# Causal attention of a two-layer kernel: two heads over the 128 rows of the array, masks added in VectorE's maximum

## The chip, the cores and the metric

The kernel runs on one NeuronCore of a Trainium2 chip. The time is the device time of one execution, in microseconds (us); three runs of the kernel before gave 1619.24, 1622.28 and 1633.52, median 1622.28.

## The reference, cut to what matters

Two transformer layers over X of 4 x 512 tokens and 256 features. Only the attention of the first layer, and the projection in front of it, are touched:

```python
Xn = (X - mu) * rsqrt(var + EPS) * ln_g + ln_b
Q, K, V = (split_heads(Xn @ W + b) for W, b in ((Wq, bq), (Wk, bk), (Wv, bv)))   # 16 heads of 16 features
scores = einsum('bhqd,bhkd->bhqk', Q, K) / sqrt(16)
scores = where(causal, scores, -inf)
A = softmax(scores, axis=-1)
AV = einsum('bhqk,bhkd->bhqd', A, V)        # then heads side by side, @ Wo + bo
```

After it come a feed-forward part with decoded 4-bit weights, a second attention (4 groups of features, no mask), and 64 experts of which each token takes 6.

## The kernel before, in words

A program of blocks. In a block each engine (PE is TensorE, DVE VectorE, ACT ScalarE, POOL GpSimd, SP the engine that issues most DMAs) has its own list of instructions, in order, and semaphores written by hand join them. The blocks that matter:

**make_constants** loads X on SP; POOL sets an identity matrix and `mask_q`, a 128 x 128 triangle of 0 and -1e30.

**project_qkv** goes over four chunks of 512 tokens (`chunks`). Each chunk is normalized on DVE (for chunk c+1 while chunk c is multiplied), transposed and multiplied on PE. Q and K are each written as a high part `hi` (fp32r, by ACT, L297) and a remainder `lo` (by DVE, L262), and V with a column of ones. SP stores them (L212, L215): per chunk four DMAs of 512 KB for `hi` and `lo` of Q and K, and one of 1 MB for V. `hi` and `lo` have one buffer each: ACT and DVE wait on `qk_stored` before they overwrite them for the next chunk. The next block starts only when all stores have landed.

**attention** (`att` in the rows) works on 16 units, each 512 tokens by 4 heads. Four buffers (SLOTS) hold the stacks of a unit. A stack holds, at 16 partitions each, the parts of Q (hi, lo, hi, lo) and of K (hi, hi, lo, lo), so that one product over them gives the whole product of the sums; eight DMAs of 128 KB load them (L461). Rows 96 and 97 hold the negated row maximum in two parts against ones in K's stack. A unit runs through these steps:

- `scores_q`: PE makes scores with queries over the partitions, block row i (128 queries) by (i+1)*128 keys, 11 groups of heads in two banks of `ps_1`, in the order i = 2, 1, 0, 3. A second matmul (L568) adds the mask on the diagonal block of each head.
- `maxima` (L701): DVE reduces a group to the row maximum. `split_maxima` (L710, L712) negates and splits it, PE turns it (`turn_maxima`, into its own bank `ps_tr`), ACT copies it, and SP writes it into Q's stack in two DMAs (L476).
- `scores_k` (L586): PE makes the transposed scores, maximum subtracted, two heads per step; `exps` on ACT (L661) takes the exponential of both at once; POOL zeroes the masked triangle (L535).
- `values` (L600): PE multiplies with V, four heads beside each other in four groups of 32 columns. ACT copies the output, PE turns it (`turn_output`), DVE normalizes it, SP stores it.

The order on PE is written by hand (`body`): one body works on four units at once, between steps of the scores_q of units u and u+1 stand those of the scores_k of u-1 and the values of u-2 and u-1. `scores_q` waits on `max_done` for a free bank; the first `scores_k` of a unit waits on `neg_loaded`, the DMAs of the maxima.

Of the kernel before, what the change touches and what calls it, by code (L numbers as in the profile page):

```python
# [7 lines left out]
F32 = mybir.dt.float32  # L8
F32R = mybir.dt.float32r
# [4 lines left out]
ALU = mybir.AluOpType  # L14
# [35 lines left out]

def make_constants(nc, x_dram, x_sb, ident, ident_bf, mask_q):

    with ExitStack() as ctx:
# [11 lines left out]
        @block.gpsimd  # L65
        def _(pool):
            for t in (ident, ident_bf, mask_q):
                pool.memset(t[:, :], 0.0).then_inc(filled, 1)
            pool.wait_ge(filled, 3)
# [4 lines left out]
            pool.affine_select(out=mask_q[:, :], in_=mask_q[:, :], compare_op=ALU.is_ge, fill=NEG, base=0,  # L74
                               pattern=[[-1, P]], channel_multiplier=1).then_inc(shaped, 1)
            pool.wait_ge(shaped, 3)

# [73 lines left out]

def project_qkv(nc, tag, x_sb, ident, w, affine, q_dram, k_dram, v_dram, heads, pitch):

# [5 lines left out]
    with ExitStack() as ctx:  # L159
# [33 lines left out]
        block = ctx.enter_context(nc.Block())  # L193
        NQ = 2 * KD

        @block.sync
        def _(sp):
# [10 lines left out]
            def body(c, more):  # L208
                for j, dst in enumerate((q_dram, k_dram)):
                    sp.wait_ge(lo_done, c * NQ + (j + 1) * KD)  # L210
                    for part, t in enumerate((hi, lo)):
                        sp.dma_start(dst[part].rearrange("(k p) t -> p k t", p=P)[:, :, bass.ds(c * CHUNK, CHUNK)],  # L212
# [5 lines left out]
            chunks(sp, body)  # L218
            sp.wait_ge(qk_stored, 16 * 4 * NCH)
            sp.wait_ge(v_stored, 16 * NCH)  # L220
# [10 lines left out]
        def _(dve):  # L231
# [23 lines left out]
            def body(c, more):  # L255
                if more:
                    norm(c + 1)
                wait(dve, qk_stored, c * 64)
                for n in range(NQ):
# [19 lines left out]
        def _(act):  # L279
# [10 lines left out]
            def body(c, more):  # L290
                if more:
                    roots(c + 1)
                wait(act, qk_stored, c * 64)
                for n in range(NQ):
# [1514 lines left out]
def program(nc, a, y):  # L1809

    with ExitStack() as ctx:
# [3 lines left out]
        ident_bf = s.sbuf("ident_bf", [P, P], BF16)  # L1815
        mask_q = s.sbuf("mask_q", [P, P], BF16)
        q_dram = nc.dram_tensor("q_parts", [2, D, T], F32, kind="Internal").ap()
        k_dram = nc.dram_tensor("k_parts", [2, D, T], F32, kind="Internal").ap()
# [3 lines left out]
        make_constants(nc, a["L0_attn_X"], x_sb, ident, ident_bf, mask_q)  # L1822

        for layer, heads, pitch, causal, parts in ((0, 16, 32, True, PARTS_16), (1, 4, 66, False, PARTS_64)):
# [4 lines left out]
            project_qkv(nc, f"qkv{layer}", x_sb, ident, w, affine, q_dram, k_dram, v_dram, heads, pitch)  # L1829
            attention(nc, f"att{layer}", ident, ident_bf, mask_q, q_dram, k_dram, v_dram, att_dram,  # L1830
                      heads, pitch, causal, parts, scale)
            if layer == 1:
# [51 lines left out]
```

## Time and profile before

| | us |
|---|---|
| three runs | 1619.24, 1622.28, 1633.52 |
| the profiled execution | 1626.69 |
| its span, first to last instruction | 1625.0 |
| projection of layer 0, up to the first load of attention | to 89.3 |
| causal attention | 89.3 to about 308 |

The profile is one execution. Busy time is what an engine spends in instructions; waits are put down to the engine or DMA whose event ended them. PE matmuls are pipelined and their ends modelled, so a busy PE may still not stream columns all the time. "Granted clock" is 1.00 for 2.4 GHz and 0.50 for 1.2 GHz.

### The profile page before, as it was taken

The page shows a single profiled execution, that of the slowest core. Times are in us where ns is not written, and L with a number is a line of the kernel's source. Part 1 is how long each engine was busy: PE and PEld are TensorE (multiplying, and loading weights), DVE is VectorE, ACT ScalarE, POOL GpSimd, SP SyncE. Part 2 cuts the span into 40 slices and gives each one's busy share as a digit, 9 for nine tenths or more (in the row PEclk, how much of TensorE's full clock was granted, in tenths as well). Part 3 has the DMA queues.
Part 4 walks back from the last instruction along what each step waited for, and adds up shares of the span by engine and source line. Part 5 has one row for each costly group of instructions (what it writes and reads, how often), then busy time and mean ns, then how long its engine had stood idle before and what let it go on. Part 6 is the DMA issues. An engine that isn't in the chain of part 4 may idle for free. (4 is left out here: it accounts for less than half of the span.)

```text
span 1625.0 us, 23544 instructions
## 1 busy us (share of the span) xinstructions
PE 1295.9 (80%) x6028; PEld 905.4 (56%) x6028; DVE 781.8 (48%) x2451; ACT 378.8 (23%) x746; POOL 383.9 (24%) x478
## 2 busy tenths in 40 slices
PE   4859999648799999796997647910999999999960
PEld 2435555436688887653554534510677677767640
DVE  6746666277412212253442564401555555655546
ACT  1205455333211212021332111100222222222210
POOL 0042222432100000001000204774233333333320
PEclk9959999879999999998999758965899999999985
DMA  3598786411980000055442201223999999999959
GB/s 109 219 178 115 119 124 94 101 52 63 295 266 1 0 0 0 23 195 174 128 132 71 69 1 56 103 110 113 276 309 308 296 299 298 312 294 297 299 177 323
DMA packets 189717, 260.04 MB, mean 160 GB/s; under 512 B 43887, under 2 KB 119375, under 8 KB 189655
## 3 DMA queue, kind: packets, MB, share of 16 engines
q1 hardware_dynamic: 141847, 190.33, 43.2%
q10 hardware_dynamic: 35568, 34.74, 7.3%
q0 software_dynamic: 12240, 34.23, 5.9%
q8 instruction: 29, 0.48, 0.1%
q14 instruction: 33, 0.27, 0.1%
HBM read 173.11 MB, written 85.78 MB: 159 GB/s over the span
## 5 line engine op out<-in xcount | busy, mean ns | idle before, releaser
L1553 PE MATMUL experts_ps_gu<-experts_wgu,experts_xt 128*128 128x352 f32 x636 | 218.4, 466 | 4.1 <-DMA experts_wgu<-L_ffn_w_gate_up 3.0
L1689 POOL DMA_INDIRECT y_parts<-experts_y,experts_at x159 | 152.6, 960 | 290.9 <-DVE experts_y L1645 287.9
L701 DVE TENSOR_REDUCE att_mx<-att_ps 128x1 f32<-128x512 f32 (+3 forms) x240 | 151.9, 654 | 135.4 <-PE att_ps L568 67.1
L564 PE MATMUL att_ps<-att_ks,att_qs 96*128 96x512 f32 (+4 forms) x384 | 157.3, 475 | 30.0 <-DMA att_ks<-k_parts 27.2
L1574 PE MATMUL experts_ps_y<-experts_wd,experts_ht 96*128 96x256 f32 x636 | 164.0, 380 | 0.0
L1596 ACT ACTIVATE experts_xt<-experts_ps_x 128x256 f32<-128x256 f32 x159 | 61.1, 384 | 417.1 <-PE experts_ps_x L1542 409.8
L661 ACT ACTIVATE att_pt<-att_ps 128x1024 f32<-128x1024 f32 (+3 forms) x160 | 121.9, 766 | 134.5 <-PE att_ps L586 134.3
L1553 PEld LDWEIGHTS experts_ps_gu<-experts_wgu,experts_xt 128*128 128x128 f32 x636 | 121.1, 192 | 49.1 <-DMA experts_wgu<-L_ffn_w_gate_up 4.3
L564 PEld LDWEIGHTS att_ps<-att_ks,att_qs 96*128 96x128 f32 (+1 forms) x384 | 78.3, 207 | 94.3 <-issue 61.4
L1542 PE MATMUL experts_ps_x<-all_ident,experts_x 128*128 128x128 f32 x318 | 64.6, 285 | 70.6 <-DMA experts_x<-x_sorted 70.6
L1383 POOL DMA_INDIRECT x_sorted<-all_rows,moe_slots x96 | 96.8, 1008 | 92.1 <-DVE moe_slots L1376 63.1
L586 PE MATMUL att_ps<-att_qs,att_ks 128*128 128x512 f32 (+3 forms) x384 | 109.4, 382 | 8.9 <-DMA att_qs<-att_neg_t 7.9
L1574 PEld LDWEIGHTS experts_ps_y<-experts_wd,experts_ht 96*128 96x128 f32 x636 | 109.9, 193 | 8.8
L600 PE MATMUL att_ps_o<-att_pt,att_vs 128*32 128x512 f32 (+4 forms) x640 | 112.9, 475 | 0.5 <-POOL att_pt L535 0.5
L1031 PE MATMUL mlp_ps_y<-mlp_w_down,mlp_inner 128*128 128x256 f32 x512 | 112.3, 382 | 0.8 <-DVE mlp_inner L949 0.8
L1031 PEld LDWEIGHTS mlp_ps_y<-mlp_w_down,mlp_inner 128*128 128x128 f32 x512 | 97.7, 191 | 14.9 <-DVE mlp_inner L949 1.3
L1655 DVE SCALAR_TENSOR_TENSOR experts_placed<-experts_x,experts_owner,experts_part 128x6 f32<-128x6 f32 x159 | 35.2, 222 | 128.7 <-DMA y_parts<-experts_y,experts_at 128.5
L949 DVE TENSOR_TENSOR mlp_inner<-mlp_gs,mlp_ps_u 128x512 f32<-128x512 f32 x64 | 43.8, 687 | 98.4 <-PE mlp_ps_u L1021 93.6
L1542 PEld LDWEIGHTS experts_ps_x<-all_ident,experts_x 128*128 128x128 f32 x318 | 50.5, 201 | 71.6 <-DVE experts_hid L1674 70.9
L1563 PEld LDWEIGHTS experts_ps_h<-all_ident,experts_hid 128*96 128x96 f32 x318 | 47.7, 173 | 72.4 <-DVE experts_hid L1630 54.3
L535 POOL TENSOR_SCALAR_AFFINE_SELECT att_pt<-att_pt 128x256 f32<-128x256 f32 x128 | 52.0, 407 | 143.6 <-ACT att_pt L661 143.4
L586 PEld LDWEIGHTS att_ps<-att_qs,att_ks 128*128 128x128 f32 x384 | 63.8, 196 | 35.1 <-issue 12.3
(202 smaller groups left out, 2051.5 us busy)
## 6 DMA issues: line engine op xcount, KB each, us to landing
experts_wgu<-L_ffn_w_gate_up SPq DMA_DIRECT2D x159, 352.0 KB, 5.6
experts_wd<-L_ffn_w_down SPq DMA_DIRECT2D x159, 176.0 KB
experts_x<-x_sorted ACTq DMA_DIRECT2D x159, 136.0 KB, 5.3
x_sorted<-mlp_w_empty SPq DMA_DIRECT2D x26, 816.0 KB, 10.6
att_qs<-q_parts SPq DMA_DIRECT2D x112, 128.0 KB, 3.3
att_ks<-k_parts SPq DMA_DIRECT2D x112, 128.0 KB, 5.3
combine_got<-y_parts ACTq DMA_DIRECT2D x24, 512.0 KB, 9.5
q_parts<-qkv_hi SPq DMA_DIRECT2D x8, 512.0 KB, 2.9
```

The lines of the kernel that those rows point to most:

```text
L564: ins = pe.matmul(out, qs[a][z][0:rows_a, h, i * P:(i + 1) * P], ks[a][z][0:rows_a, h, 0:width(i)], start=a == 0, stop=a == last_part and ...
L586: ins = pe.matmul(out, ks[a][z][:, h, jj * P:(jj + 1) * P], qs[a][z][:, h, off(jj):S], start=a == 0, stop=a == last_part)
L600: ins = pe.matmul(ps_o[h * pitch:(h + 1) * pitch, off(j):S], vs[z][:, j, h * pitch:(h + 1) * pitch], pt[:, j * hu + h, 0:S - off(j)], star ...
L661: act.activation(pt[:, 2 * n:2 * n + 2, 0:w], ps_2[:, n % 2, :, 0:w], ACT.Exp, scale=scale).then_inc(exp_done, 1)
L701: dve.tensor_reduce(mx[:, hs[0]:hs[-1] + 1, i], ps_1[:, (u.c * ng + g) % 2, 0:len(hs) * width(i)] .rearrange("p (h w) -> p h w", h=len(hs) ...
L1031: ins = pe.matmul(ps_y[:, i % 2, 0:D], inner[0:r, m, i * P:(i + 1) * P], w_down(m), start=m == 0, stop=m == nm - 1)
L1383: pool.indirect_dma_start(out=self.dram[:, :], out_offset=bass.IndirectOffsetOnAxis(ap=self.slots[:, k, i:i + 1], axis=0), in_=self.rows[: ...
L1542: ins = pe.transpose(ps_x[:, k * P:(k + 1) * P], x[u.slot][:, k:D:KD], ident[:, :])
L1553: ins = pe.matmul(ps_gu[:, u.bank, 0:2 * FE], xt[:, u.bank, k, :], wgu[u.slot][:, k, :], start=k == 0, stop=k == KD - 1)
L1574: ins = pe.matmul(ps_y[:, u.bank, 0:D], ht[u.c % 2][:, k, :], wd[u.slot][:, k, :], start=k == 0, stop=k == 1)
L1596: act.activation(xt[:, u.bank, :, :], ps_x[:, 0:KD * P].rearrange("p (k t) -> p k t", k=KD), ACT.Copy)\
L1689: pool.indirect_dma_start(out=parts_dram[:, :], out_offset=bass.IndirectOffsetOnAxis(ap=at[u.slot][:, 0:1], axis=0), in_=y[u.slot][:, :], ...
```

## The change

Causal attention becomes a function of its own, `causal_attention`; the second layer keeps the old one. What it does:

- **Stores.** For layer 0, Q and K are stored ready stacked: `q_dram` is [16 heads, 48, tokens], three parts of 16 rows a head (`Q_PARTS` hi, hi, lo; `K_PARTS` hi, lo, hi; the product lo by lo is gone). Per chunk these are 12 DMAs of 256 KB instead of 4 of 512 KB.
- **Stacks.** Two heads lie over the partitions, at 0 and at 64, 48 rows each, and the two rows of the maximum behind them. Four DMAs of 192 KB load a unit. POOL first sets the whole of K's stack to 1, and the first load of each buffer waits on it.
- **scores_q, scores_k** are issued in pairs, one matmul on partitions 0 to 47 (49), one on 64 to 111 (113), into two banks. `ps_1` has three banks, and takes the turned maxima and the turned output too.
- **Masks.** `WIDE = ()`: no mask on PE. DVE takes for each head and each i a `tensor_tensor_reduce`: add the mask (`mask_wide`, 512 wide, fp32 in SBUF), write the sum, give its maximum. 16 of them a unit in place of 11 reductions.
- **Order.** The body keeps its steps. New waits: the pair of i = 1 waits on `neg_copied`; every pair on the maxima that read its banks; the turned output on all of i = 1. The maxima go out in four DMAs.

```diff
+                    for place, part in enumerate(stacked[j] if stacked else ()):
+                        t = (hi, lo)[part]
+                        for k in range(KD):
+                            rows = dst[k * heads // KD:(k + 1) * heads // KD, place * hd:(place + 1) * hd, :]
+                            sp.dma_start(rows[:, :, bass.ds(c * CHUNK, CHUNK)],
+                                         t[:, j, k, :].bitcast(F32)).then_inc(qk_stored, 16)
...
-PARTS_16 = [(((0, 0), (16, 1), (32, 0), (48, 1)), ((0, 0), (16, 0), (32, 1), (48, 1)))]
+Q_PARTS, K_PARTS = (0, 0, 1), (0, 1, 0)
+WIDE = ()
...
+                if not u.plus(-SLOTS).exists():
+                    sp.wait_ge(ones_set[z], 1)
+                for dram, stack in ((q_dram, qs), (k_dram, ks)):
+                    for m in range(2):
+                        src = dram[bass.ds(g * hu, hu), :, bass.ds(b * S, S)].rearrange("(r m) d t -> m d r t", m=2)
+                        sp.dma_start(stack[z][m * half:m * half + of_parts, :, :].bitcast(F32), src[m])\
+                            .then_inc(qk_loaded[z], 16)
...
+                for m in range(2):
+                    for r in range(2):
+                        row, first = m * half + neg_row + r, (2 * m + r) * 2 * CT
+                        sp.dma_start(qs[u.slot][row:row + 1, :, :].bitcast(F32),
+                                     neg_t[first:first + 2 * CT, :]).then_inc(neg_loaded[u.slot], 16)
...
+                for a, r in enumerate(each):
+                    for m in range(2):
+                        at = slice(m * half, m * half + of_parts)
+                        ins = pe.matmul(outs[m][:, a * w:(a + 1) * w], qs[z][at, r, i * P:(i + 1) * P],
+                                        ks[z][at, r, 0:w], start=i not in WIDE, stop=i not in WIDE or a == len(each) - 1)
+                ins.then_inc(s1_done, 1)
...
+                scores_q(u, 3, 0, 0, maxima(8))
+                scores_k(v, 0, 0)
+                values(t, 2)
+                scores_q(u, 3, 1, 2, maxima_and_output(9))
+                scores_k(v, 0, 1)
+                scores_q(w, 2, 0, 4, maxima(11))
+                scores_k(v, 1, 0)
+                values(t, 3)
+                scores_q(w, 2, 1, 6, maxima(13))
+                scores_k(v, 1, 1)
+                turn_maxima(u, maxima(14))
+                scores_q(w, 1, 0, 10, maxima_and_copy(16))
+                scores_k(v, 2, 0)
+                values(v, 0)
+                scores_k(v, 2, 1)
+                scores_q(w, 0, 0, 12, maxima(17))
+                scores_k(v, 3, 0)
+                turn_output(t, before_output)
+                values(v, 1)
+                scores_k(v, 3, 1)
...
+                        wait(dve, max_done, done - 1 + m)
+                        for a, r in enumerate(each):
+                            ins = dve.tensor_tensor_reduce(
+                                out=masked_scores[:, m, a * w:(a + 1) * w], in0=bank[:, a * w:(a + 1) * w],
+                                in1=mask_wide[:, S - w:S], scale=1.0, scalar=NEG, op0=ALU.add, op1=ALU.max,
+                                accum_out=mx[:, m, r, i:i + 1])
```

## Rows read from the trace of the kernel before

**Rows 1.** The page: span, and busy time of engines.

```profile
span 1625.0 us, 23544 instructions
PE 1295.9 (80%) x6028; PEld 905.4 (56%) x6028; DVE 781.8 (48%) x2451; ACT 378.8 (23%) x746; POOL 383.9 (24%) x478
```

**Rows 2.** Busy time by stage: stretch, length, engines, granted clock, DMA share, GB/s.

```profile
36.60:89.30 52.70, 40.45 (x133) 23.79 (x131) 35.03 (x103) 11.32 (x19) 0.00 (x0) 0.91 0.65 239
89.30:99.60 10.30, 0.00 (x0) 0.03 (x1) 3.53 (x2) 0.00 (x0) 10.14 (x6) 0.50 0.97 135
99.60:141.40 41.80, 39.85 (x206) 24.94 (x206) 26.54 (x48) 13.22 (x20) 13.74 (x20) 0.71 0.94 126
141.40:284.00 142.60, 139.31 (x1009) 80.12 (x1010) 91.53 (x178) 75.00 (x119) 38.30 (x95) 1.00 0.80 115
284.00:308.00 24.00, 18.82 (x148) 9.04 (x147) 6.24 (x15) 12.86 (x22) 7.59 (x19) 1.00 0.10 23
```

**Rows 3.** Who waited for whom, 150 to 300 us: total, times, longest.

```profile
ACT att_pt L661 <- PE att_ps L586: 68.2, 86, 1.9
DVE att_mx L701 <- PE att_ps L568: 45.0, 69, 1.6
PE att_ps L586 <- DMA att_qs<-att_neg_t: 2.2, 4, 0.7
```

**Rows 4.** The timeline around the stores, and the first memset of attention.

```profile
36.65 0.40 SPq L212 DMA_DIRECT2D q_parts<-qkv_hi  x1
...
76.58 1.27 ACT L297 ACTIVATE qkv_hi<-qkv_ps_qk,qkv_bqk 128x512 fp32r<-128x512 f32 x2 [6.49 <-DMA k_parts<-qkv_lo]
...
78.81 0.38 SPq L212 DMA_DIRECT2D q_parts<-qkv_hi  x1
...
...
89.34 1.80 POOL L509 MEMSET att_qs<- 64x2048 f32 x1 [76.72 <-POOLq L159]
```

**Rows 5.** One window of the last chunk's stores, columns as in group 2.

```profile
87.00:88.00 1.00, 0.00 (x0) 0.00 (x0) 0.00 (x0) 0.00 (x0) 0.00 (x0) 0.50 1.02 377
```

**Rows 6.** DMA packets at 379.8-384.2 (scales, 8 leading rows), then 384.2-387.8 (codes, 128).

```profile
DMA packets 136, 0.26 MB, mean 60 GB/s; under 512 B 8, under 2 KB 8, under 8 KB 136
...
DMA packets 144, 0.26 MB, mean 73 GB/s; under 512 B 16, under 2 KB 16, under 8 KB 144
```

**Rows 7.** Windows in loads onto 16 partitions (causal attention), and onto 64 (second).

```profile
93.00:94.00 1.00, 0.00 (x0) 0.00 (x0) 0.85 (x1) 0.00 (x0) 1.00 (x1) 0.50 1.09 131
749.50:750.50 1.00, 0.00 (x0) 0.00 (x0) 0.00 (x0) 0.00 (x0) 0.08 (x1) 0.50 1.04 216
```

**Rows 8.** VectorE by shape, whole span: count, busy us, mean ns, idle before.

```profile
L701 DVE TENSOR_REDUCE att_mx<-att_ps 128x1 f32<-128x512 f32 x128 | 85.6, 689 | 92.3 <-PE att_ps L564 66.1 <-PE att_ps L568 25.9
L701 DVE TENSOR_REDUCE att_mx<-att_ps 128x1 f32<-128x384 f32 x64 | 33.0, 554 | 12.1 <-PE att_ps L568 10.3
L1658 DVE SCALAR_TENSOR_TENSOR experts_picked<-experts_x,experts_owner 128x6 f32<-128x6 f32 x159 | 35.0, 220 | 0.0
L1658 DVE DVE_READ_ACCUMULATOR experts_picked<-experts_x,experts_owner 128x1 f32 x159 | 13.0, 82 | 0.0
```

**Rows 9.** The timeline of one unit: a score weight load, weights and products of a values step.

```profile
209.21 0.19 PEld L586 LDWEIGHTS att_ps<-att_qs,att_ks 128*128 128x128 f32 x1
...
209.64 0.16 PEld L600 LDWEIGHTS att_ps_o<-att_pt,att_vs 128*32 128x32 f32 x8 [0.20 <-issue]
209.64 1.06 PE L600 MATMUL att_ps_o<-att_pt,att_vs 128*32 128x512 f32 x8
```

**Rows 10.** Issues by line, 95 to 306 us: count, KB each, us to landing.

```profile
att_qs<-att_neg_t SPq DMA_DIRECT2D x32, 8.0 KB, 3.6
```

**Rows 11.** Windows where the clock stayed low, and where it fell; columns as in group 2.

```profile
107.00:109.50 2.50, 2.38 (x7) 1.28 (x7) 1.95 (x3) 0.00 (x0) 0.41 (x1) 0.50 1.19 180
...
760.00:762.00 2.00, 1.49 (x6) 1.24 (x7) 0.04 (x1) 0.25 (x1) 0.00 (x0) 1.00 0.54 164
762.00:764.00 2.00, 2.00 (x6) 1.54 (x5) 1.38 (x2) 0.77 (x1) 0.00 (x0) 0.53 0.68 205
```

More of the change, by code:

```diff
@@ L72, in _ @@
                                    pattern=[[-1, P]], channel_multiplier=1).then_inc(shaped, 1)
-            pool.affine_select(out=mask_q[:, :], in_=mask_q[:, :], compare_op=ALU.is_ge, fill=NEG, base=0,
+            for width in (P, 2 * P):
+                for a in range(0, S, width):
+                    diagonal = mask_q[:, width // P - 1, a + width - P:a + width]
+                    pool.affine_select(out=diagonal, in_=diagonal, compare_op=ALU.is_ge, fill=NEG, base=0,
+                                       pattern=[[-1, P]], channel_multiplier=1).then_inc(shaped, 1)
+            diagonal = mask_wide[:, S - P:S]
+            pool.affine_select(out=diagonal, in_=diagonal, compare_op=ALU.is_ge, fill=NEG, base=0,
                                pattern=[[-1, P]], channel_multiplier=1).then_inc(shaped, 1)
-            pool.wait_ge(shaped, 3)
+            pool.wait_ge(shaped, 2 + 4 + 2 + 1)
 def wait(eng, sem, n):
@@ L194, in project_qkv @@
         NQ = 2 * KD
+        n_stores = sum(len(parts) * KD for parts in stacked) if stacked else 4
         @block.sync
@@ L210, in body @@
                     sp.wait_ge(lo_done, c * NQ + (j + 1) * KD)
-                    for part, t in enumerate((hi, lo)):
+                    for place, part in enumerate(stacked[j] if stacked else ()):
[4 more added lines that the diff above has]
+                                         t[:, j, k, :].bitcast(F32)).then_inc(qk_stored, 16)
+                    for part, t in enumerate(() if stacked else (hi, lo)):
                         sp.dma_start(dst[part].rearrange("(k p) t -> p k t", p=P)[:, :, bass.ds(c * CHUNK, CHUNK)],
@@ L218, in _ @@
             chunks(sp, body)
-            sp.wait_ge(qk_stored, 16 * 4 * NCH)
+            sp.wait_ge(qk_stored, 16 * n_stores * NCH)
             sp.wait_ge(v_stored, 16 * NCH)
@@ L257, in body @@
                     norm(c + 1)
-                wait(dve, qk_stored, c * 64)
+                wait(dve, qk_stored, c * 16 * n_stores)
                 for n in range(NQ):
@@ L292, in body @@
                     roots(c + 1)
-                wait(act, qk_stored, c * 64)
+                wait(act, qk_stored, c * 16 * n_stores)
                 for n in range(NQ):
@@ L1821, in program @@
         sorted_dram = nc.dram_tensor("x_sorted", [NSLOT, ROW], F32, kind="Internal").ap()
-        make_constants(nc, a["L0_attn_X"], x_sb, ident, ident_bf, mask_q)
-        for layer, heads, pitch, causal, parts in ((0, 16, 32, True, PARTS_16), (1, 4, 66, False, PARTS_64)):
+        make_constants(nc, a["L0_attn_X"], x_sb, ident, ident_bf, mask_q, mask_wide)
+        for layer, heads, pitch in ((0, 16, 32), (1, 4, 66)):
+            stacked = (Q_PARTS, K_PARTS) if layer == 0 else None
+            q_dram, k_dram = (nc.dram_tensor(f"{n}{layer}_parts", [heads, len(Q_PARTS) * D // heads, T] if stacked
+                                             else [2, D, T], F32, kind="Internal").ap() for n in "qk")
             w = {n: a[f"L{layer}_attn_{n}"] for n in ("Wq", "bq", "Wk", "bk", "Wv", "bv", "Wo", "bo")}
@@ L1828, in program @@
             scale = (D // heads) ** -0.5 if layer == 0 else SCALE_1
-            project_qkv(nc, f"qkv{layer}", x_sb, ident, w, affine, q_dram, k_dram, v_dram, heads, pitch)
-            attention(nc, f"att{layer}", ident, ident_bf, mask_q, q_dram, k_dram, v_dram, att_dram,
-                      heads, pitch, causal, parts, scale)
+            project_qkv(nc, f"qkv{layer}", x_sb, ident, w, affine, q_dram, k_dram, v_dram, heads, pitch,
+                        stacked)
+            if layer == 0:
+                causal_attention(nc, "att0", ident, ident_bf, mask_q, mask_wide, q_dram, k_dram, v_dram, att_dram,
+                                 heads, pitch, scale)
+            else:
+                attention(nc, "att1", ident, ident_bf, None, q_dram, k_dram, v_dram, att_dram, heads, pitch, False,
+                          PARTS_64, scale)
             if layer == 1:
```

298 lines of the change are left out of this document (291 added, 7 removed).

## The prediction

> **What bounds the kernel now.** I read the page's busy times first: PE is busy 80% of 1625.0 us, DVE 48% [rows 1]. That is an average over stages, and the change touches only two of them, so the stages come next [rows 2]. The projection of layer 0 stores from 36.6 to 89.3. Causal attention first waits 10.3 us for its stacks (no PE at all, DMA share 0.97), then fills its pipeline until 141.4, then runs steadily to 284, then drains. In the steady stretch ACT issues 10 instructions a unit, so 119 are 11.9 units in 142.6 us: a period of 12.0 us. PE is busy 139.3 of the 142.6, DVE 91.5, which is 7.7 a unit.
>
> What the period waits for is in the waits [rows 3]: ACT on the transposed scores (68.2 us in 150), DVE on the masked scores (45.0). The reader is to see a hand-to-hand chain between PE, DVE and ACT, with PE the busiest; the DMA of the maxima ends only 2.2 us of it. So the steady stretch is bound by PE's order, and a cheaper PE helps as long as DVE, with 4.3 us a unit to spare, can pay for it.
>
> The other end is the timeline of the stores [rows 4]. The last chunk's `hi` could not be written before the chunk before it had landed: ACT idled 6.49 us for `k_parts<-qkv_lo` at 76.58. Q's store follows 2.2 us later (78.81), and attention begins at 89.34. In between the DMA engines are full: 377 GB/s at share 1.02 [rows 5]. Earlier chunks hide their stores: a chunk stores 3.1 MB, 8.3 us at 377, and first stores begin at 36.65 and the last at 78.81, so three intervals take 42.2 us, 14.1 each. What is stored counts fully behind chunk 2 and chunk 3, and elsewhere only beyond some 14 us.
>
> **The change, part by part.**
>
> *Stores.* A chunk stored 2.1 MB of Q and K and stores 3.1 MB now (12 x 0.262), and V's 1.05 as before. At 377 GB/s the extra 1.05 MB is 2.8 us, twice on the path: +5.5 us. That is the lower bound. The upper one comes from the form. The destination of each new DMA is 8 heads x 16 rows x 512, the old one 128 x 2 x 512. The kernel before has one DMA with 8 leading rows (the scales, 8 x 16 x 512) and a like one with 128 (the codes), both 256 KB. Beside the same 128 packets of data the scales' have 8 packets under 512 B and the codes' 16 [rows 6]. I read those as the completion writes of each DMA engine that took part, so 8 against 16 engines. If all 12 stores lie on the same eight, they run at half of 377, 189 GB/s: 3.15 MB take 16.7 us. Now no chunk hides them. First data come about 1 us after the issue, at 37.6; Q and K of chunk 0 are down at 54.3. `hi` of the next chunk starts then, its store follows 2.2 us later and about 0.9 to the first data, while V's 2.8 us drain on these engines: a cycle of 16.7 + 3.1 = 19.8. So chunk 3 is down at 54.3 + 3 x 19.8 = 113.7, V 2.8 later, and attention begins about 1 us after that, at 117.5 instead of 89.3: +28 us. SP's 13 issues a chunk at 0.4 each are 5 us and hide behind that. Rows show eight engines for such a DMA, not that it is always the same eight; nothing in the trace speaks for a spread, so I take +28 and keep +5.5 as the other end.
>
> The Trainium skill ("DMA: Bandwidth & Descriptors", section "Why a DMA increments its semaphore by 16 and not by 1") says that the number of engines is the largest divisor up to 16 of both patterns' slowest dimension, and that a DMA issued by SP takes the lowest-numbered ones. By it the twelve stores share eight engines and the sum stays at +28; the trace agrees as far as the 8 against 16 small packets go.
>
> *Loads.* A unit loaded 1.05 MB of Q and K at 131 GB/s, and this onto 16 partitions per DMA; the second attention gets 216 onto 64 partitions [rows 7]. 0.79 MB now go onto 48. At 131 a unit takes 6.0 us, at 216 3.6, in place of 8.0. POOL's ones come first: 1.80 for 2048 elements [rows 4], so 0.9 for 1024. In the first 10.3 us this gives +0.9 - 2.0 to +0.9 - 4.4; in the filling the next units' loads shrink as well, but DVE's chain takes over there. I take -4 us (48 partitions are nearer to 64). In the steady stretch loads are hidden, before and after.
>
> *Masks and maxima on DVE.* 512 elements cost 689 ns, 384 cost 554 [rows 8]: 1.05 ns an element, 150 fixed. Before, 11 reductions with 5120 elements a unit are 7.0 us. After, there are 16 with the same 5120. If a `tensor_tensor_reduce` costs what a reduction does, this is 5.4 + 2.4 = 7.8 us. The nearest row with an accumulated output is a 6-element operation of 220 ns followed by a READ_ACCUMULATOR of 82: 300 fixed, 150 more each, 10.2 us for 16. `split_maxima` has two instructions more, +0.3. A gain is excluded: it does what the reduction does, and more. I take 0.82 for 512 elements (0.685, 0.55, 0.42 for the narrower), since this is the only kind of row with such an output: 9.9 a unit, 11.7 with split and normalize. DVE becomes the engine with the least to spare.
>
> *PE.* 16 mask matmuls go, and 32 score matmuls become 16 pairs. If the two of a pair run side by side, a pair takes PE about 0.25 (one weight load of 0.19 [rows 9] plus streaming not covered); if they follow each other, 0.4. The trace shows such overlap only for groups of columns: eight loads of V's weights lie within 0.16 us, and eight products of 512 columns within 1.06 [rows 9]. I take side by side.
>
> The Trainium skill ("TensorE: Matmul & The Clock Gate", Part 3, "The mechanism") states overlap for row groups too, weight loads included; no row here shows it, and by it the pair is 0.25, the value taken anyway.
>
> *The period.* I follow one body from the moment (0) at which `scores_k` 1,1 is issued. i = 1 now waits for ACT's exponential of 1,1 and its copy of the maxima, two at a mean of 0.63 (75.00 / 119 [rows 2]), plus hand-overs: 1.45. PE behind it is blocked, scores_k 2,0 and `values` too. Then PE's own chain: six pairs' worth of i = 1, scores_k 2,0 and 2,1 and i = 0 (1.35), values 1.06 + 0.2, scores_k 3,0 0.25, turned output 0.8, values 0.85 + 0.2, scores_k 3,1 0.25, and 0.5 until DVE has i = 3: together 5.5. Then DVE's: four of 0.82, split 0.9, one of i = 2 0.685, after which the second pair of i = 2 (its bank free) and scores_k 1,1 are issued, 0.55. Sum 1.45 + 5.5 + 4.85 + 0.55 = 12.35 against 12.0. With the low price of DVE it is 11.7. Over some 13 steady units: +4.6 (low price -4).
> The maxima's DMAs are hidden: four issues from 1.45 on and 3.6 us to land [rows 10] are there before 7.2, when scores_k 0,0 wants them.
>
> *Rest.* The drain is PE and ACT alone, with cheaper pairs: -2. The longer constants on POOL lie beside the load of X, 10 us; uncovered they'd cost some 2.
>
> **Sum**: +28 - 4 + 4.6 - 2 = +26.6 on the profiled 1626.7, 1653. The profiled execution lies 4.4 above the median of the runs, so I give 1622.3 + 26 = **1648 us**.
>
> **Rivals.**
>
> *R1, PE gets slow, 1656 to 1685 (0.22).* Either the pairs do not overlap: 0.15 more on eight pairs of the 5.5 chain and on two at its end, 1.5 a unit, x 13 = +20, 1668. Or the clock falls. The filling stretch stayed at 0.50 with PE busy 2.38 of 2.50 in short pieces, and the clock fell at 762 after PE was busy 1.49 of 2.00 [rows 11]. After the change PE has some 8 us of work in 12.35, with waits of 1.3 us before and after scores_k 1,1. If each unit loses a few us at half clock, that is 1 to 2.5 a unit, +13 to +33. For it: less work on PE. Against it: the dense 5.5 us each unit.
>
> *R2, the stores spread over all engines, 1622 to 1630 (0.13).* +5.5 instead of +28: 1622.3 + 4 = 1626. For it: no row shows twelve such DMAs in flight. Against it: the eight small packets.
>
> *R3, attention gives it back, 1610 to 1626 (0.12): the other side.* DVE at the low price has 9.55 us of work a unit (7.8 + 1.75). If PE's earlier pairs and the third bank end DVE's waits, the period nears that: 9.6 is 2.4 less x 13 = -31, against +28 - 6: 1613. It decides from a period of 10.3 down (22 / 13 = 1.7 below 12.0). For it: DVE's 45 us of waiting on PE. Against it: the new wait on `neg_copied`, and the banks that hand over one by one.
>
> *R4, R2 and R3 together, 1585 to 1605 (0.05)*: 1622 + 5.5 - 6 - 31 = 1591.
>
> **How the numbers follow.** The forecast (eight engines, full clock, period 11.7 to 12.7) has 0.45: 1640 to 1656. The remaining 0.03 is for what I don't see. The range of 8 in 10 leaves out R4, the lower part of R3 and the upper end of R1: 1618 to 1680. About 1% is what a measurement can tell from no change, 1606 to 1638.5. Below it: R4 and little else, 0.06. Within: R2, R3, 0.24. Above: forecast and R1, 0.70.
>
> **What would show it.** Stores: the first load of attention near 117 (near 95 if R2), DMA share about 0.5 between 38 and 113, ACT waiting on stores in chunks 1 to 3. Loads: PE's first scores about 6 us after that. DVE: 0.72 to 0.82 us for 512 elements, 9.5 to 11.7 busy a unit. Period: SP's stores of the output 12.3 apart, DVE idle under 1 us a unit, PE waiting for ACT before i = 1. The forecast is wrong if the share stays near 1 in the stores, if the clock is not 1.00 after 150, or if the two matmuls of a pair start a weight load apart.

## The result, and the profile after

| | before | after |
|---|---|---|
| median, us | 1621.26 (1619.24 to 1633.52, four runs) | 1682.49 (1676.76 to 1684.91, four runs) |
| profiled execution, us | 1626.69 | 1676.76 |
| its span | 1625.0 | 1674.9 |
| first store of Q | 36.65 | 37.20 |
| first load of attention | 89.34 | 125.89 |
| first load of the output projection | 308.08 | 365.72 |
| low clock within attention | 34.5 | 188.6 |

The changed kernel takes 1.036 of the time before, 95% interval 1.030 to 1.041: 61 us more, where I had forecast 26 with a range up to 1680. The two profiled spans differ by 49.9: projection +36.6, attention +21.1 (239.8 against 218.7), everything behind it -7.7. That last part is untouched by the change; the profile of before lies 5 us above its median and that of after 6 below. Ratios, here and in the table of experiments, leave out executions more than 1.5% above the fastest of their kernel.

Windows of the kernel after, by stage, with the columns of [rows 2] (PE, PEld, DVE, ACT, POOL busy, granted clock, DMA share, GB/s):

```profile
37.20:125.90 88.70, 41.10 (x130) 23.74 (x128) 34.75 (x102) 10.93 (x19) 0.99 (x2) 0.75 0.54 190
125.90:133.00 7.10, 0.69 (x2) 0.29 (x2) 0.18 (x1) 0.00 (x0) 2.65 (x3) 0.50 0.86 191
133.00:178.10 45.10, 30.15 (x161) 13.69 (x161) 30.02 (x141) 15.07 (x23) 6.85 (x17) 0.58 0.44 96
178.10:341.00 162.90, 136.24 (x806) 60.29 (x810) 99.01 (x449) 72.96 (x118) 38.04 (x94) 0.59 0.35 80
341.00:366.00 25.00, 19.37 (x139) 7.60 (x131) 5.73 (x19) 12.34 (x21) 6.81 (x17) 0.77 0.10 22
...
61.00:63.00 2.00, 2.00 (x4) 0.69 (x3) 1.93 (x8) 0.00 (x0) 0.00 (x0) 0.50 0.47 139
71.00:73.00 2.00, 2.00 (x11) 1.67 (x9) 1.93 (x6) 0.00 (x0) 0.00 (x0) 1.00 0.53 203
77.00:79.00 2.00, 0.00 (x0) 0.00 (x0) 0.00 (x0) 0.29 (x1) 0.00 (x0) 0.96 1.02 368
259.60:266.50 6.90, 4.92 (x45) 1.87 (x43) 5.52 (x19) 4.04 (x6) 1.93 (x5) 0.99 0.62 130
266.50:273.30 6.80, 6.00 (x34) 2.79 (x34) 3.64 (x22) 2.23 (x5) 1.62 (x4) 0.51 0.29 46
```

Two things are to be seen. While Q and K are stored, 203 GB/s move at a DMA share of 0.53; in V's store behind them it is 368 at 1.02. And the steady stretch of attention, which ran at clock 1.00 before [rows 2], runs at a mean of 0.59. ACT's 118 instructions are 11.8 units in 162.9 us, 13.8 us a unit against 12.0.

The timeline of SP for the second of the four chunks, and that of ACT (in brackets its idle time and what ended it):

```profile
59.10 3.48 SPq L224 DMA_DIRECT2D q_parts<-qkv_hi  x4
62.77 3.02 SPq L224 DMA_DIRECT2D q_parts<-qkv_lo  x2
66.00 2.32 SPq L224 DMA_DIRECT2D k_parts<-qkv_hi  x2
68.42 2.75 SPq L224 DMA_DIRECT2D k_parts<-qkv_lo  x2
71.27 2.25 SPq L224 DMA_DIRECT2D k_parts<-qkv_hi  x2
73.81 0.94 SPq L230 DMA_DIRECT2D v<-qkv_vs  x1
81.00 1.99 SPq L224 DMA_DIRECT2D q_parts<-qkv_hi  x2
...
56.79 2.42 ACT L312 ACTIVATE qkv_hi<-qkv_ps_qk,qkv_bqk 128x512 fp32r<-128x512 f32 x4 [9.23 <-DMA k_parts<-qkv_hi]
78.71 2.42 ACT L312 ACTIVATE qkv_hi<-qkv_ps_qk,qkv_bqk 128x512 fp32r<-128x512 f32 x4 [9.74 <-DMA k_parts<-qkv_hi]
```

One store of Q follows the other at 21.9 us. Q and K need 19.6 of them (59.10 to 78.71). SP takes 0.9 to 1.5 us for an issue, where the issues of [rows 4] took 0.4. V's store is issued at 73.81 and runs behind K's.

The waits of the kernel after, 180 to 330 us (total, times, longest):

```profile
ACT att_pt L1058 <- PE att_ps L962: 84.0, 73, 2.5
DVE att_masked_scores L1107 <- PE att_ps L943: 52.1, 49, 1.6
PEld att_ps L943 <- DVE att_mx L1107: 41.7, 40, 1.8
```

In the same 150 us ACT and DVE wait for PE longer than before (84.0 and 52.1 against 68.2 and 45.0 [rows 3]), though PE has less to do. The timeline of PE shows why, with the same steps at the two clocks:

```profile
261.98 0.49 PE L943 MATMUL att_ps<-att_ks,att_qs 48*128 48x512 f32 x2
...
266.08 0.28 PE L995 MATMUL att_ps<-all_ident,att_neg 128*32 128x128 f32 x1
267.30 0.79 PE L943 MATMUL att_ps<-att_ks,att_qs 48*128 48x256 f32 x4 [0.93 <-ACT att_neg_t L1075]
...
268.24 1.93 PE L976 MATMUL att_ps_o<-att_pt,att_vs 128*32 128x512 f32 x8
```

The `values` of 512 columns takes 1.93 us where it took 1.06 [rows 9]. The 0.93 in front of the pair of i = 1 is the new wait for the copied maxima. A unit's stores of the output lie 14.6 us apart where the whole unit is at the low clock, and 12.4 where a stretch of some 7 us is at the high one (259.6 to 266.5 above).

DVE and the pairs, from the timelines of DVE and of PE's weight loads:

```profile
218.38 0.69 DVE L1107 CUSTOM_DVE_ANT_0 att_masked_scores<-att_ps,all_mask_wide 128x512 f32<-128x512 f32 x1 [1.62 <-PE att_ps L943]
218.99 0.09 DVE L1107 DVE_READ_ACCUMULATOR2_ANT att_mx<- 128x1 f32 x1
218.99 0.69 DVE L1107 CUSTOM_DVE_ANT_0 att_masked_scores<-att_ps,all_mask_wide 128x512 f32<-128x512 f32 x1
...
...
261.98 0.19 PEld L943 LDWEIGHTS att_ps<-att_ks,att_qs 48*128 48x128 f32 x2 [0.47 <-DVE att_mx L1107]
```

The next masked maximum starts 0.61 us after the one before, and the read of the accumulator costs nothing of its own. Two weight loads of a pair lie in 0.19 us: the pairs do run side by side.

The same operations of DVE grouped by shape, 90 to 370 us (count, busy us, mean ns, idle before):

```profile
L1107 DVE CUSTOM_DVE_ANT_0 att_masked_scores<-att_ps,all_mask_wide 128x512 f32<-128x512 f32 x64 | 41.6, 688 | 28.4 <-PE att_ps L943 28.4
L1107 DVE CUSTOM_DVE_ANT_0 att_masked_scores<-att_ps,all_mask_wide 128x384 f32<-128x384 f32 x64 | 33.1, 555 | 34.7 <-PE att_ps L943 31.4 <-issue 3.0
...
L1107 DVE DVE_READ_ACCUMULATOR2_ANT att_mx<- 128x1 f32 x256 | 21.2, 83 | 0.0
```

### The profile page after: what moved, and what is told of

It is laid out like the page before. It is cut to its first block and busy times, and to the rows that moved or that the text cites. A ratio compares the mean times of both kernels' runs of the same rounds, so it can differ in the third digit from the quotient of the medians.

```text
span 1674.9 us, 23414 instructions
## 1 busy us (share of the span) xinstructions
PE 1281.0 (76%) x5772; PEld 876.0 (52%) x5772; DVE 792.3 (47%) x2817; ACT 377.5 (23%) x746; POOL 372.6 (22%) x479
## 5 line engine op out<-in xcount | busy, mean ns | idle before, releaser
L1107 DVE CUSTOM_DVE_ANT_0 att_masked_scores<-att_ps,all_mask_wide 128x384 f32<-128x384 f32 (+3 forms) x256 | 112.9, 488 | 101.7 <-PE att_ps L943 98.3
L943 PE MATMUL att_ps<-att_ks,att_qs 48*128 48x384 f32 (+3 forms) x256 | 62.1, 530 | 79.5 <-DMA att_ks<-k_parts 37.6
L1058 ACT ACTIVATE att_pt<-att_ps 128x1024 f32<-128x1024 f32 (+3 forms) x128 | 89.1, 704 | 115.4 <-PE att_ps L962 114.8
L943 PEld LDWEIGHTS att_ps<-att_ks,att_qs 48*128 48x128 f32 x256 | 33.9, 287 | 110.3 <-DVE att_mx L1107 64.3
L2052 DVE COPY experts_ht<-experts_ps_h 96x256 f32<-96x256 f32 x159 | 66.9, 421 | 35.8 <-issue 20.4
L1402 ACT ACTIVATE mlp_gs<-mlp_ps_g 128x512 f32<-128x512 f32 x64 | 37.5, 596 | 181.5 <-PE mlp_ps_g L1435 181.4
L2059 DVE TENSOR_SCALAR experts_y<-experts_ps_y,experts_share 128x256 f32<-128x256 f32 x159 | 75.7, 476 | 1.5 <-PE experts_ps_y L1988 1.5
```

Source lines behind the costliest of these rows:

```text
L943: ins = pe.matmul(outs[m][:, a * w:(a + 1) * w], qs[z][at, r, i * P:(i + 1) * P], ks[z][at, r, 0:w], start=i not in WIDE, stop=i not in WI ...
L1058: act.activation(pt[:, 2 * n:2 * n + 2, 0:w], ps_2[:, n % 2, :, 0:w], ACT.Exp, scale=scale).then_inc(exp_done, 1)
L1107: ins = dve.tensor_tensor_reduce(out=masked_scores[:, m, a * w:(a + 1) * w], in0=bank[:, a * w:(a + 1) * w], in1=mask_wide[:, S - w:S], sc ...
L2052: dve.tensor_copy(ht[u.c % 2][:, :, :], ps_h[0:FPAD, 0:2 * P].rearrange("p (k t) -> p k t", k=2))\
L2059: dve.tensor_scalar(y[u.slot][:, :], ps_y[:, u.bank, 0:D], share[u.slot][:, 0:1], None, ALU.mult)\
```

## The experiments

All were timed beside the kernel before. "Low clock" is the time in attention at the lower level, and "unit" the time between two stores of the output; both, like the lengths, are those of the one profiled execution.

| run | ratio to before (95%) | attention from, length | low clock | unit |
|---|---|---|---|---|
| changed kernel | 1.036 (1.030 to 1.041) | 125.9, 239.8 | 188.6 | 14.6, some 12.4 |
| e1_rows16 | 1.017 (1.009 to 1.025) | 96.4, 245.4 | 207.9 | mostly 14.6 |
| e8_no_masks | 1.015 (1.009 to 1.020) | 94.3, 240.4 | 192.7 | 14.1 to 14.8, some 12.1 |
| e4_masks_on_pe | 1.074 (1.065 to 1.082) | 124.9, 307.9 | 284.0 | 18.4, two of 16.5 |
| e2_k_twice | 1.046 (1.039 to 1.053) | 124.6, 261.4 | 213.6 | 14.0 to 16.4 |
| e3_both_twice | 1.047 (1.039 to 1.055) | 125.9, 246.2 | 99.4 | 13.6 |
| e6_q_twice | 1.023 (1.017 to 1.028) | 95.7, 243.0 | 133.7 | 13.6 |
| e5_values_first | 1.003 (1.000 to 1.006) | 94.7, 219.4 | 134.1 | 10.2 or 14 |
| e7_values_first_q_twice | 1.002 (0.999 to 1.005) | 96.0, 233.2 | 120.5 | 11 to 16 |
| e9_k11_early | 0.996 (0.991 to 1.002) | 94.2, 205.2 | 92.6 | 10.1, two of 12 to 14 |
| e10_k11_thrice | 0.989 (0.979 to 0.999) | 94.9, 216.7 | 121.1 | 10.1 to 13.8 |
| e11_values_first_k_twice | 0.997 (0.993 to 1.000) | 95.8, 217.7 | 94.8 | 10.6 to 14.4 |
| e12_full_filler | 0.990 (0.987 to 0.994) | 94.8, 193.2 | 39.6 | 10.1 to 10.3 |
| e15_half_filler | 0.990 (0.986 to 0.994) | 95.7, 193.7 | 47.0 | 10.1, two of 12 |
| e13_full_filler_all | 1.010 (1.006 to 1.013) | 95.2, 227.7 | 36.5 | 12.3 |
| e16_rows48_filler | 1.004 (1.001 to 1.007) | 95.7, 224.1 | 132.0 | 11.7 to 13.7 |
| e14_after_filler | 1.010 (1.006 to 1.013) | 126.2, 193.2 | 36.2 | 10.2 |

**e1: the stores on more engines.** The three parts of a head lie interleaved in DRAM (row = 3 x feature + part), so that the destination is 128 equal steps instead of 8 heads x 16 rows. The same bytes, the same 12 DMAs.

```diff
-rows = dst[k * heads // KD:(k + 1) * heads // KD, place * hd:(place + 1) * hd, :]
+rows = dst[k * heads // KD:(k + 1) * heads // KD].rearrange(
+    "h (d n) t -> (h d) n t", n=len(stacked[j]))[:, place, :]
```

> The changed kernel, with the 48 rows of a head stored in another order (row = 3 x feature + part, for Q and K alike, so that the products are the same sums). The destination of each store then steps evenly over 128 rows instead of 8 x 16; number, size and bytes of the stores stay. Theory (eight leading rows leave half of the DMA engines out): DMA share goes from 0.53 to about 1 in the stores, attention's first load comes about 30 us earlier (near 95 instead of 125.9), and the time is 1682 - 30 = 1652. Rival (it is the number of stores, 12 of them at 1.2 us of issue each, or the extra megabyte): share stays near 0.5, the first load comes at 115 or later, the time is 1672 or more.

Two windows of e1 within its stores:

```profile
45.00:46.00 1.00, 1.00 (x4) 0.45 (x3) 0.93 (x4) 0.00 (x0) 0.00 (x0) 1.00 1.02 363
59.00:60.00 1.00, 1.00 (x4) 0.52 (x3) 0.70 (x5) 0.00 (x0) 0.00 (x0) 1.00 1.04 381
```

The share doubles, attention starts at 96.4 instead of 125.9, and the median falls from 1682 to 1655.44. The eight engines are shown as the cause of 29.5 of the 36.6 us. What stays against before is 7.1: 0.5 from a later first store, 0.95 for the first ones on POOL, and 5.6 of stores, close to the 0.9 and +5.5 that I had for these two.

**e8: the masks off DVE.** On e1, twelve plain reductions a unit, one for each half of a pair; the mask is left out of the maxima (and of nothing else).

```diff
-                    if i in WIDE:
+                    if True:
```

> The kernel with interleaved rows (e1) in which the row maxima leave the causal mask out: VectorE takes 12 plain reductions of unmasked scores instead of 16 additions with a maximum. It leaves out the mask of the maxima only (the exponentials are still masked by GpSimd). Theory (clock, with TensorE's chain the bound): VectorE saves well under 1 us a unit and little of it is on the path, the period stays within 0.5 of 14.6. Rival (the masks on VectorE made the period longer than before): it falls to 13 or less.

1651.67, 4 us under e1, which is less than the two intervals are wide. At this mostly low clock DVE's masks were at most a small part of what attention waited for. At the high clock no run prices them; there DVE is busy 8.31 of a unit's 10.10 us (e12 below), close behind PE.

**e4: the masks on PE.** On the changed kernel, one bf16 matmul per head on its diagonal, and plain reductions.

```diff
+                    for m in range(2):
+                        ins = pe.matmul(outs[m][:, a * w + i * P:(a + 1) * w], ident_bf[:, :],
+                                        mask_q[:, 0, 0:P], start=False, stop=True)
```

> The changed kernel with one part undone: all masks are again added on TensorE (a bf16 matmul on the diagonal block of each head), and VectorE takes plain reductions, 12 a unit. Theory of the clock: the 16 more full-array matmuls keep the clock up more often, the mean granted clock in attention rises from 0.59 and the period falls below 14. If instead VectorE's masks were what costs: VectorE's busy time falls by about 1 us a unit, the clock stays where it is and the period falls by that, to 13.3. If neither holds: period 14.5 or more, the masks being work on the path at half clock (0.2 to 0.3 x 16).

1748.21: the unit grows from 14.6 to 18.4 us, and the clock is low almost throughout. On the changed kernel masks on PE cost more than on DVE. One unit of e4:

```profile
205.25:223.94 18.69, 17.81 (x89) 7.15 (x85) 7.83 (x18) 6.27 (x10) 3.25 (x8) 0.50 0.26 65
```

PE is busy 95% of it, its sixteen mask matmuls cover all 128 rows and columns, and still the clock is 0.50 all through. Why they did not raise the clock here, when four do below, I have not found out: sixteen of 128 columns are as many columns as four of 512, but they stand two at a time between the pairs of 48 rows, and those of e12 and e14 one behind the other.

**e2, e3, e6, e7: pairs issued twice.** Doubled are scores_k (e2), both (e3), scores_q on e1 (e6), scores_q on e5 (e7). Outputs unchanged.

```diff
-                for m in range(2):
+                for m in (0, 1, 0, 1):
```

> The changed kernel, with every pair of scores_k matmuls issued twice, the second over the first (same result): 16 more matmuls and weight loads a unit. Theory (TensorE's clock is what attention lost: it ran at 0.50 more than at 1.00, and a unit took 14.6 us at 0.50): the clock stays at 1.00 for longer, the steady period is 12.5 or less, attention 10 to 25 us shorter in spite of the work. Rival (the new waits set the period and the clock follows from them): the added work comes on top, 0.25 to 0.4 for each of 8 pairs, period 15 to 17, attention 20 to 40 us longer.

> As the one before, and scores_q twice as well. Theory of the clock: granted clock near 1.00 throughout the steady stretch, period about 12, attention 20 to 35 us shorter than in the changed kernel. Rival: longer by the added work, period 17 or more.

> The kernel with interleaved rows (e1), every scores_q pair issued twice (same result). With both kinds twice the clock held at 1.00 and a unit took 13.6. Theory of the clock: with half of that extra work the clock may still hold; then the period is 12.5 to 13 and attention 225 to 235 instead of 245. If the clock does not hold it is 15 to 16, as with scores_k twice, and attention 255 or more.

> The two edits before this one together (interleaved rows, values step first, scores_q twice). If idle time on TensorE is what keeps the clock down, this has the least of it: clock 1.00 through the steady stretch, period 12.0 to 12.5, attention 215 to 225, time about 1635. Rival: period no lower than in either of the two alone.

Doubling scores_k (e2) made attention 21.6 us longer, as the rival said. Adding e3's second doubling to e2's costs nothing: 1701.03 and 1700.75. The unit gets shorter though PE has more to do, because the low clock halves from 213.6 us to 99.4. So PE's own work is not what bounds the unit; the level of its clock is. In e3 and e6 nearly every steady unit takes 13.6 us. The clock did not hold in e3, though e6's expectation says that it did: in every such unit it is low for 3.4 us in e3 and for 6.8 in e6. Why the two come to the same length I can't say. e7 puts e6's doubling on e5 and brings nothing over e5 (1.002 and 1.003); its theory of a steady high clock fell.

**e5: an order with less waiting.** On e1, `values(v, 0)` goes ahead of the pairs of i = 1 and fills the 0.93 us.

```diff
+                values(v, 0)
                 scores_q(w, 1, 0, 10, maxima_and_copy(16))
                 scores_k(v, 2, 0)
-                values(v, 0)
```

> The kernel with interleaved rows (e1) and one step moved on TensorE: the first values step of unit v stands ahead of the i = 1 scores, which wait for ScalarE's copy of the maxima, instead of behind them. Theory (TensorE waits 0.8 to 1.0 us a unit for that copy, and its idle time keeps the clock down): the values step, 1.9 us at half clock, covers the wait; the period falls from 14.6 by about 1, to 13.6, and more if the clock rises: e1's attention of 245 becomes 225 or less. Rival (the i = 1 scores and VectorE behind them come later by as much as TensorE wins): the period stays at 14 to 15.

1631.91, level with before. Its profile holds both regimes side by side: five units of 10.1 to 10.2 us at the high clock from 172 to 223, then units of about 14 after it has fallen. At the high clock the changed attention is faster than the old one by 1.8 us a unit.

**e9, e10, e11: more work for PE in tiles of 48 rows.** e9 moves scores_k 1,1 ahead of the second pair of i = 2, where PE waited 1.28 us for DVE; e10 issues it three times; e11 is e5 with all scores_k twice.

```diff
+                scores_k(v, 1, 1)
                 scores_q(w, 2, 1, 6, maxima(13))
-                scores_k(v, 1, 1)
```

> On top of e5 (stores on 16 engines, values of a unit's first keys ahead of the scores of i = 1), scores_k 1,1 moves ahead of the second pair of i = 2. In e5 PE idled 1.28 us for VectorE in front of that pair and ScalarE idled 0.87 us for scores_k 1,1, so the step fits into the hole. Theory (attention is set by the clock, and the clock by how long PE idles): the hole of 1.28 us becomes about 0.9, more of the attention runs at the high clock, some units of 10.2 us or a little less in place of 14: about 1615, ratio 0.995. Rival (the clock doesn't follow one order of steps, it changes by itself): the same mix of 10.2 and 14 us units as e5, 1625 to 1640, ratio 1.00.

> As e9, but the two matmuls of scores_k 1,1 are issued three times, into the same bank, so that PE works through the 1.28 us in which it waited for VectorE. Output unchanged. Theory (PE's idle time costs the clock): clock 1.00 over most of the attention, units of 10.2 to 10.8 us throughout, attention 190 to 200 us against 219 in e5: about 1605, ratio 0.985. Rival (the clock falls with the share of the array that works, and pairs of 48 rows do not count as full work): clock still low for half of the attention, and the added matmuls cost at the low clock 0.8 us a unit: 1640, ratio 1.01.

> e5 with each pair of scores_k issued twice. Output unchanged. Adds some 8 x 0.3 = 2.2 us of PE at the high clock to units whose PE is busy 7.6 of 10.2. Theory (idle time costs the clock): the clock stays high, units of 11 to 12 us throughout: attention about 200 us, 1610 to 1620. Rival: clock low half the time as in e7, units of 11 to 16: 1635 to 1645, ratio 1.005.

e9 has a median of 1626.81 over eight executions from 1613.82 to 1657.95; its low clock of 92.6 us is from one of the fastest (1614.27). The mean granted clock of the whole kernel is 0.847 to 0.857 in e1's executions and 0.867 to 0.876 in e5's; in e9's it is 0.845 to 0.880, so what e9 adds to e5 is not settled. e11 brings the low clock of e5 down from 134.1 to 94.8, but not its attention (217.7 against 219.4), where I had expected 200. e10 was to test e9 with PE's hole filled: its profile, at 1629.57, has 121.1 us of low clock, but its four executions run from 1599.82 to 1635.50, so neither its ratio nor that profile decides anything.

**e12, e15, e13: work over the whole array.** On e9, matmuls of the mask against the identity (bf16, 128 rows, 512 wide) into the bank that scores_k then overwrites: four in front of 1,1 (e12), two (e15), two in front of every scores_k (e13).

```diff
+                if n == 3:
+                    for m in (0, 1, 0, 1):
+                        pe.matmul(ps_2[:, n % 2, m, 0:S], ident_bf[:, :], mask_q[:, 0, :], start=True, stop=True)
```

> As e9, with four extra matmuls of the mask against the identity (bf16, all 128 rows and columns, 512 wide) in front of scores_k 1,1, into the bank that it then overwrites: about 0.85 us at the high clock, in the hole where PE waited 1.28 us for VectorE. Output unchanged. Compare with e10, whose filler took about as long in tiles of 48 rows and left 121 us of low clock in its profile. Theory A (PE's idle time and the share of the array that works set the clock; tiles of 48 rows weigh little): low clock under 60 us of the attention, units of 10.2 to 10.8, 1600, ratio 0.985 and steady. Theory B (such fillers don't raise the clock): low clock 90 to 130 us as in e9 to e11, 1625 to 1635, ratio 1.00.

> e12 with two of the four filler matmuls (about 0.43 us at the high clock). Output unchanged. If two are enough to hold the clock: units of 10.1, low clock about 40 us, 1611 as e12, ratio 0.990. If the clock needs all four: falls come back in some units, low clock 70 to 100 us, 1618 to 1626, ratio 0.995 to 1.00, wider spread.

> As e9, with two such full-array matmuls (512 wide, bf16) ahead of every pair of scores_k: 8 x 0.43 = 3.4 us of PE a unit at the high clock. Output unchanged. Theory A (share of the array): clock 1.00 in nearly all of the attention after its filling, units of 11 to 12.2 us throughout, attention 200 to 210 us, 1615, ratio 0.993. Theory B: low clock over 90 us; the filler costs 6.8 us a unit at the low clock, units of 14 to 18, 1650 or more, ratio 1.02.

**e16: the same four on 48 rows.** One thing more differs from e12: all four go into one bank, where e12's alternate between two.

```diff
-                    for m in (0, 1, 0, 1):
-                        pe.matmul(ps_2[:, n % 2, m, 0:S], ident_bf[:, :], mask_q[:, 0, :], start=True, stop=True)
+                    for _ in range(4):
+                        pe.matmul(ps_2[:, n % 2, 0, 0:S], ident_bf[0:48, :], mask_q[0:48, 0, :], start=True, stop=True)
```

> e12 with the same four filler matmuls cut to 48 rows of the array (identity and mask from partitions 0 to 47; 128 columns and 512 elements wide as before, all into one bank), so PE is busy for as long as in e12 and idle for as long. Output unchanged. Theory (the share of the array's rows that works counts for the clock): low clock over 80 us of the attention as in e9 and e10, 1620 to 1630, ratio 0.995 to 1.00. Rival (only busy time counts, and e10's filler was too short or of the wrong type): low clock about 40 us, units of 10.1, 1611, ratio 0.990 as e12.

The window 150 to 280 of e9, e12 and e16, in this order:

```profile
150.00:280.00 130.00, 104.53 (x830) 46.22 (x834) 97.51 (x447) 74.64 (x122) 40.36 (x99) 0.89 0.45 96
```

```profile
150.00:280.00 130.00, 110.54 (x928) 47.68 (x925) 98.40 (x450) 80.77 (x131) 42.35 (x104) 1.00 0.46 97
```

```profile
150.00:280.00 130.00, 116.22 (x766) 51.27 (x762) 87.40 (x398) 64.39 (x104) 33.87 (x83) 0.73 0.40 94
```

With the full-array matmuls the clock is 1.00 all through and ACT gets 131 instructions done; with the same number on 48 rows it is 0.73, and ACT gets 104. PE's busy times here can't be compared, because the same work lasts longer at the low clock. So here are a unit of e12, a unit of e15, and the last 10.2 us of e16 before its clock falls at 209.1, all three at 1.00:

```profile
193.54:203.64 10.10, 8.72 (x75) 3.79 (x75) 8.31 (x38) 6.25 (x10) 3.26 (x8) 1.00 0.58 118
180.63:190.72 10.09, 8.19 (x72) 3.59 (x73) 8.31 (x38) 6.18 (x10) 3.26 (x8) 1.00 0.62 123
198.90:209.10 10.20, 8.58 (x74) 3.86 (x73) 8.43 (x41) 6.35 (x11) 3.27 (x9) 1.00 0.35 98
```

PE is as busy in e16 as in e12 within 0.14 us, and busier than in e15, and its clock falls all the same, seven times between 150 and 300. So busy time alone does not hold the clock. What differs is the rows of the array that the added work covers, and the bank, which no run tells apart from the rows. Every execution bears this out: the mean granted clock of the whole kernel is 0.891 to 0.899 in e12's six and 0.853 to 0.877 in e16's twelve. The filler itself shortens nothing: e9 has units of 10.1 to 10.3 without it wherever its clock is high.

e12, which does useless work, is 1.0% faster than the kernel before, and e15 shows that two matmuls a unit do nearly as well (1611.31, with one fall of the clock in its profile). e13 holds the clock as well, but PE is then busy all 70 of 70 us (170 to 240) and the unit is 12.3.

**e14: the changed kernel itself with e12's filler.** Stores and order as changed; the four matmuls stand ahead of the second pair of i = 2.

```diff
+                filler(v, 2)
                 scores_q(w, 2, 1, 6, maxima(13))
                 scores_k(v, 1, 1)
```

> The changed kernel itself, stores and order untouched, plus the filler of e12 (four bf16 matmuls of the mask against the identity, 128 x 128 x 512, into a bank of scores_k) ahead of the second pair of i = 2, where PE waits for VectorE. Output unchanged. Stores stay at eight engines, so attention starts near 126 as in the changed kernel. Theory (the fall of the clock is the whole of the attention's loss, and PE's work over the full array prevents it): low clock under 60 us in place of 188.6, units of 10.5 to 11.5 in place of 12.4 to 14.6, attention near 200 against 239.8, 1645, ratio 1.012: less than the forecast of the change. Rival (in this order the wait on the copied maxima and the low clock both cost): low clock over 100 us, units of 12 to 14, 1665 or more.

The window 170 to 300 of the changed kernel, then of e14:

```profile
170.00:300.00 130.00, 110.24 (x643) 48.19 (x642) 77.53 (x350) 57.16 (x92) 29.60 (x74) 0.58 0.37 84
```

```profile
170.00:300.00 130.00, 105.29 (x916) 48.24 (x927) 105.74 (x480) 78.41 (x127) 41.01 (x102) 1.00 0.50 105
```

1642.91 us. Attention is 193.2 long instead of 239.8, with the wait on the copied maxima still in it (0.93 us a unit). So the low clock costs the change 46.6 us in its profile, and 39.6 by the medians (1682.49 and 1642.91). The mean granted clock is 0.882 to 0.892 in e14's seven executions and 0.841 to 0.848 in the four of the changed kernel.

## Why the prediction was wrong

The sum in the prediction's terms, as the profiles give it: stores and ones +36.6, attention at the high clock 193.2 - 218.7 = -25.5 (e14), the low clock +46.6, the rest of that execution -7.7: together +50.0, the difference of the two spans. For attention I had -4 + 4.6 - 2 = -1.4; that 1682 still lies close to the end of my range is luck, since -25.5 and +46.6 were both missed and largely cancel.

- *Stores (+28): mechanism right, mis-sized by 8.4 (36.6 against 28.2).* Eight engines, as e1 shows. The Trainium skill ("DMA: Bandwidth & Descriptors", section "Why a DMA increments its semaphore by 16 and not by 1") gives eight for a slowest dimension of 8, and trace and e1 agree (share 0.53, then 1.02). The term that failed is the 16.7 us for Q and K of a chunk; from the first issue it took 19.6, so 18.7 without the 0.9 to the first data that I had counted apart. The plateau of 203 GB/s is better than my 189, but it isn't held from the start: in the second chunk the window 61 to 63 moves 139 GB/s at a share of 0.47. SP was then taking 0.9 to 1.5 us an issue; whether its issues held the transfers back, or full queues held the issues, no run tells. The 2.2 behind it was 2.3 (78.71 to 81.00). Three cycles took 65.4 (37.20 to 102.61) in place of 59.4, the last chunk with POOL's ones 1.8 more than I gave it, and the first store came 0.55 later: 8.4.
- *Loads (-4): near.* PE's first scores come 6.2 us after the first load (the forecast said about 6), in place of the 10.3 of [rows 2], at 191 GB/s, between the 131 and 216 of [rows 7]. POOL's ones, 1.0 us, were in my -4 and lie in the stores here, so the term is -3.1.
- *Masks on DVE (0.82 us for 512): too dear.* The lower end was right: 0.688 busy, 0.61 from start to start. The row I leaned on, a 6-element operation followed by the read of an accumulator [rows 8], was like in form; but here that read overlaps the next operation. At the mostly low clock e8 prices the whole of it at about 4 us.
- *PE's pairs side by side: right*, at 0.19 for both weight loads at the high clock, 0.28 at the low one.
- *The period (12.35): wrong twice over.* At the high clock it is 10.25 in e14, just at the 10.3 from which I had let R3 decide. By e14's timeline from the pair of i = 1 (209.03) to the first of i = 3 (212.71) PE takes 3.7 us where I summed 5.0 (5.5 with the hand-over to DVE): I added 0.2 to each `values` and 0.25 for each pair, where they overlap one another. From there to the second pair of i = 2 (217.51) it is 4.8 against 4.85, though DVE's operations are cheaper, since the hand-over to DVE (0.5 in my 5.5) lies in it. The rest is 1.8 against 2.0.
- *The clock: the step that decided.* I kept 1.00 and gave the fall to R1, at "a few us of each unit", +13 to +33. It fell for most of most units, 46.6. R1's clock branch was the one that happened, on top of R3's shorter period, which I had as excluding it. I had argued "against it: the dense 5.5 us each unit", from rows in which PE's busy time stood beside the clock [rows 11]. Busy time was the wrong measure: in e16 PE is busy 8.58 of the 10.20 us before a fall, in e15 8.19 of 10.09 in a unit without one, and in e4 17.81 of 18.69 at a clock of 0.50. The Trainium skill ("TensorE: Matmul & The Clock Gate", Part 1) says that the gate follows how busy PE has been of late; e5, with less idle time and a low clock of 134.1 us against e1's 207.9, agrees with it; e16 beside e12, and e4, do not.
- *The signs named in advance* did their work: the share near 0.5, ACT waiting on stores, the clock "not 1.00 after 150". The last was named as what would make the forecast wrong. The result, 1682.49, is within the bounds I had given R1 (to 1685), but the range was cut at 1680 and no case combined slow stores, a slow clock and larger terms.

Why the clock stayed high in the kernel before is not tested by itself. Its transposed scores and its masks ran over all 128 rows ([rows 9] has one such weight load) and its scores over 96, where the changed kernel has tiles of 48 to 50:

```profile
99.57 0.29 PEld L564 LDWEIGHTS att_ps<-att_ks,att_qs 96*128 96x128 f32 x1 [16.33 <-issue]
```

PE also had hardly an idle moment (139.31 of 142.60 [rows 2]). Both changed at once. e5 against e1 shows more of the high clock with less waiting, e12 against e16 that the rows (or the bank) matter; e4 shows that neither a busy PE nor full rows are enough by themselves. What the rule is, stays open.

## What to carry to other kernels

When a change takes work away from TensorE, by tiles of few rows or by moving masks elsewhere, price the kernel at both clocks before choosing a forecast: here the unit was 10.2 us at the one and 14.6 at the other. Do so though its busy share looks high: that did not tell the two apart. If the clock falls, first fill PE's holes with steps from elsewhere in the order (e5), then try a few full-array matmuls, one behind the other, into a bank about to be overwritten (e12, e15). And look at the DRAM side of each store's pattern: 8 heads x 16 rows cost 29.5 us against 128 equal steps for the same bytes.

## What the runs showed of the hardware

- Four matmuls of 128 rows a unit, one behind the other, kept the granted clock at 1.00; the same four on 48 rows and into one bank left it at a mean of 0.73, though PE was as busy before it fell (8.58 of 10.20 us against 8.72 of 10.10; e12, e16). The time is 0.990 of before against 1.004.
- Sixteen matmuls of 128 rows and 128 columns, spread over the unit, left the clock at 0.50 with PE busy 17.81 of 18.69 us (e4).
- A `tensor_tensor_reduce` of VectorE takes 688, 555, 420 and 287 ns for 512, 384, 256 and 128 elements, a plain reduction's time [rows 8], with its accumulator read (83 ns) hidden under the next one.
- The two weight loads of a pair together take 0.19 us at the high clock and 0.28 at the low; eight products of 512 columns 1.06 and 1.93.
- Loads onto 48 partitions ran at 191 GB/s. Stores on eight engines reached 203 where sixteen reach 363 to 381, and SP's issues took 0.9 to 1.5 us each meanwhile.
